# A fused Perceiver block on one core: query weights loaded first, self-attention two slots later, two products split into halves

## The reference, cut to what matters

```
x = x + cross_attention(layernorm(x), ctx)   # 16 heads, keys and values from 1601 context rows a batch
x = x + self_attention(layernorm(x))         # 8 query heads, one key and one value head of 64, causal
x = x + ffn(layernorm(x))                    # 2 shared experts, and top 2 of 8 routed ones by gates = x @ rW + rb
```

## Time and profile before

| what | before |
|---|---|
| median of 3 runs | 1284.3 us (1282.82 to 1285.09) |
| the profiled execution's own time | 1284.68 us |
| its span, first to last instruction | 1283.0 us |
| mean granted TensorE clock | 0.999 of full speed |
| PE busy | 1265.1 us, 99% of the span |
| DVE, ACT, POOL busy | 648.8, 634.0, 437.6 us |

### The profile page before, as it was taken

The page is one execution under the profiler, slowest core; times in us unless marked ns, Lnnn a source line. Parts: engine busy times, 40 slices in busy tenths (PEclk is TensorE's granted clock), DMA queues, the critical chain, the costliest instruction groups (busy, mean ns, idle before and its releaser), DMA issues.

```text
span 1283.0 us, 29915 instructions
## 1 busy us (share of the span) xinstructions
PE 1265.1 (99%) x13126; PEld 1098.9 (86%) x13126; DVE 648.8 (51%) x936; ACT 634.0 (49%) x1085; POOL 437.6 (34%) x203
## 2 busy tenths in 40 slices
PE   8999999999999999999999999999999999999998
PEld 8888888888788888788888878798989999999997
DVE  5343353443363363463453354756776555565555
ACT  3545554454545544545544536646545444554443
POOL 2345345544555545645456535200022000100000
PEclk9999999999999999999999999999999999999999
DMA  6121011012011003012003111674556499999990
GB/s 216 72 89 67 18 55 39 33 42 92 19 63 67 18 22 133 18 59 71 18 22 115 67 50 49 232 294 164 173 190 205 154 335 359 354 347 337 356 402 36
DMA packets 32775, 174.89 MB, mean 136 GB/s; under 512 B 5944, under 2 KB 8152, under 8 KB 14464
## 3 DMA queue, kind: packets, MB, share of 16 engines
q1 hardware_dynamic: 30896, 168.16, 35.6%
q0 software_dynamic: 1744, 4.76, 1.1%
HBM read 166.84 MB, written 6.06 MB: 135 GB/s over the span
## 4 chain that ended last, share of the span: by engine, by line
PE 87%; POOL 3%; DMA 3%; issue 2%; DVE 2%; ACT 2%; SPq 0%; DVEq 0%; POOLq 0%; ACTq 0%
PE bank L728 20%; PE bank L740 18%; PE bank L1079 11%; PE sc L1096 8%; PE sc L756 7%; PE sc L941 6%; PE bank L960 3%; PE bank L769 3%; PE sc L960 3%; DMA wqt<-in_aq 2%; POOL xn L587 2%; PE bank L833 1%; DMA wqt<-in_wq 1%; POOL xa L599 1%; ACT tt L1208 1%
## 5 line engine op out<-in xcount | busy, mean ns | idle before, releaser
L587 POOL TENSOR_TENSOR xn<-xn,tt 128x1024 f32<-128x1024 f32 x96 | 230.2, 2398 | 339.3 <-DVE tt L1325 338.3
L1208 ACT ACTIVATE tt<-sc 128x512 f32<-128x512 f32 (+1 forms) x208 | 107.8, 603 | 360.3 <-PE sc L756 360.2
L1423 DVE TENSOR_TENSOR wsl<-ring,wsh 128x2048 fp32r<-128x2048 f32 x72 | 166.8, 2316 | 111.6 <-ACT wsh L1163 111.1
L1312 DVE TENSOR_SCALAR kk<-bank,bkt 128x512 f32<-128x512 f32 (+2 forms) x130 | 80.8, 622 | 232.4 <-PE bank L728 232.2
L728 PE MATMUL bank<-cxh,wkh 128*128 128x512 f32 (+2 forms) x512 | 181.4, 354 | 1.5 <-DVE va L1320 1.0
L728 PE MATMUL bank<-cxl,wkh 128*128 128x512 f32 (+2 forms) x512 | 174.7, 341 | 0.0
L728 PE MATMUL bank<-cxh,wkl 128*128 128x512 f32 (+2 forms) x512 | 174.2, 340 | 0.0
L740 PE MATMUL bank<-wvh,cxh 128*128 128x512 f32 (+1 forms) x416 | 163.6, 393 | 0.0
L740 PE MATMUL bank<-wvl,cxh 128*128 128x512 f32 (+1 forms) x416 | 162.9, 391 | 0.0
L740 PE MATMUL bank<-wvh,cxl 128*128 128x512 f32 (+1 forms) x416 | 162.3, 390 | 0.0
L1163 ACT CAST wsh<-ring 128x2048 fp32r<-128x2048 f32 x72 | 137.4, 1908 | 48.2 <-PE sc L1096 20.9
(11 more groups left out here) (270 smaller groups left out, 2027.9 us busy)
## 6 DMA issues: line engine op xcount, KB each, us to landing
ring<-in_w SPq DMA_DIRECT2D x112, 1024.0 KB, 7.0
ctxt<-in_ctx SPq DMA_DIRECT2D x15, 1024.0 KB, 4.9
ctxt<-in_ctx SPq DMA_DIRECT2D x8, 642.0 KB, 3.9
ctxt<-in_ctx SPq DMA_DIRECT2D x10, 512.0 KB, 3.5
wqt<-in_wo SPq DMA_DIRECT2D x4, 1024.0 KB, 4.9
wqt<-in_aq SPq DMA_DIRECT2D x4, 1024.0 KB, 8.4
wqt<-in_ap_ SPq DMA_DIRECT2D x4, 1024.0 KB, 7.0
yrows<-K SPq DMA_DIRECT2D x1, 2048.0 KB, 9.2
```

The lines of the kernel that those rows point to most:

```text
L587: e.tensor_tensor(dacc[0:kn, y, :], dacc[0:kn, y, :], tt[0:kn, w, :], ALU.add).then_inc(s["da_pool"], 1)
L1208: e.activation(weights_view(m, kn, hb), score_read(m, kn, hb), ACT.Relu, scale=-1.0).then_inc(s["t_act"], 1)
L1423: e.tensor_tensor(wsl[m % 3][:], ring[slot(unit_split(m))][:], wsh[m % 3][:].bitcast(F32), ALU.subtract).then_inc(s["wl_dve"], 1)
```

## The change

Four edits. SP loads `in_wq` ahead of `in_wv`. `slot_of` moves every step of tiles 0 to 2 by two slots (6 becomes 8), save the gates of tile 2, which stay at slot 104. The second `halved` slot is that of step 6 instead of 5, so the split of `in_ap_` moves by three slots. The values of self-attention and the gates are made by eight products in place of four: two of 64 stationary columns each, which write PSUM partitions 0 to 63 and 64 to 127; the values are also 64 columns wide instead of 128 (the other 64 were a copy that nothing read), and so is the copy to `V2`. Both edits hold for all four tiles.

```diff
-    return next((t for t in range(3) if slot == (slot_of(t, 0) - 5, slot_of(t, 5))[what]), None)
+    return next((t for t in range(3) if slot == (slot_of(t, 0) - 5, slot_of(t, 6))[what]), None)
...
-    return 2 * PER * t + 2 * PER + 6 + (9 if d == 10 else d)
+    return 2 * PER * t + 2 * PER + 8 + (9 if d == 10 else d)
...
+            e.dma_start(wqt[:], wq).then_inc(s["wq_in"], 16)
             e.dma_start(wvt[:], wv).then_inc(s["wv_in"], 16)
-            e.dma_start(wqt[:], wq).then_inc(s["wq_in"], 16)
...
                 for c in range(4):
-                    m = e.matmul(dst[:, 0:8], xaT[:, c, :], rwt[:, c, :], start=(c == 0), stop=(c == 3))
+                    for h in range(2):
+                        r = slice(64 * h, 64 * h + 64)
+                        m = e.matmul(dst[r, 0:8], xaT[:, c, r], rwt[:, c, :], start=(c == 0), stop=(c == 3))
...
                 for c in range(4):
-                    m = e.matmul(dst[:, P:2 * P], xaT[:, c, :], avt[:, c, :], start=(c == 0), stop=(c == 3))
+                    for h in range(2):
+                        r = slice(64 * h, 64 * h + 64)
+                        m = e.matmul(dst[r, P:P + 64], xaT[:, c, r], avt[:, c, 0:64], start=(c == 0), stop=(c == 3))
...
-                e.tensor_copy(V2[:], src[:, P:2 * P]).then_inc(s["proj_read"], 1)
+                e.tensor_copy(V2[:, 0:64], src[:, P:P + 64]).then_inc(s["proj_read"], 1)
```

## The result

| what | before | after |
|---|---|---|
| median | 1283.56 us (1282.73 to 1285.09, 4 runs) | 1298.91 us (1297.9 to 1299.16, 4 runs) |
| ratio | | 1.0117 [1.0099, 1.0134] |
| span of the profiled execution | 1283.0 us | 1297.4 us |
| mean granted TensorE clock | 0.999 | 0.989 |

The account below looks back on a forecast made before the run. PE was taken as the bound, busy 1265.1 of 1283.0 us. Terms -3.5 - 2.0 + 1.4 - 3.7 + 3.2 - 2.4 = -7.0 us gave a forecast of 1277.4 us, range 1273.6 to 1282.4.

Parts of the forecast that it names:

- The step that failed: Loads of `in_ap_` and `in_wo`: claimed to have slots to spare on ACT and POOL and to cost nothing.
- (e): Rival: `context_lo` of span 0 gets behind PE at r = 10, kernel slower, some 1288 us; chance 0.05.
- The start: First loads: queries start at 15.2 instead of 16.71 us and the clock does not fall, together -3.5 us.
- the clock's 1.96 us: First sixteen query records at the start: 3.45 us at full clock instead of 5.41, a gain of 1.96 us.
- The waits of step 2, step 13 and `in_aq`: Shifted self-attention: step 2's wait gone, -2.0; step 13's grows, +1.4; `in_aq`'s gone, -3.7 us.
- The wait at `attended`: Second `attended` product waits for DVE's read of values: 1.45, 1.45 and 0.3 us, +3.2, bounds 0 and 6.0.
- The halves: Self-attention's values and gates by 64-column products side by side: 0.65 and 0.70 us, -2.4 us over four tiles.
- The gates' term: Gates made by 64-column products: 0.70 us instead of 0.95, -0.25 us a tile in four tiles.
- Rival (b): The 64-column products do not overlap: whole change -0.6 us, 1283.7 us, no change; chance 0.13.
- the dear bound: 64-column products without any overlap: 0.114 us a record, 1.8 us for values, 1.07 for gates, +3.9 us in all.
- The sum: Whole kernel: -3.5 - 2.0 + 1.4 - 3.7 + 3.2 - 2.4 = -7.0 us, forecast 1277.4 us, chance 0.52.

Follow-up runs that it names:

- e10: Changed kernel with the first split of a tile (POOL's split of wo) one slot later, residue 4 in place of 3; 1278.29 us, ratio 0.996.
- e2: Kernel before with only the output weights' split moved from r = 1 to r = 3; 1301.44 us, ratio 1.014.
- e4: Kernel before with only self-attention's values and gates made by two 64-column products side by side, with the narrower copy; 1281.38 us, ratio 0.9985.
- e5: Kernel before with only the shift by two slots, the output weights' split kept at r = 1; 1280.5 us, ratio 0.9985.
- e3: Kernel before with only the query weights loaded ahead of the value weights; 1280.94 us, ratio 0.9984.
- e6: Changed kernel with POOL's split subtraction in four instructions of 512 columns instead of one of 2048; 1290.26 us, ratio 1.0055.
- e1: Changed kernel with the output weights' split back at r = 1 instead of r = 3; 1278.11 us, ratio 0.9956.
- e12: Changed kernel with 76 idle products ahead of the value products at each of the three 4.2 us stops; 1289.35 us, ratio 1.0053.

## Why the prediction was wrong, point by point

**The step that failed** is the sentence "The loads of `in_ap_` and `in_wo` have slots to spare on ACT and POOL, and cost nothing." It is true of when the split's result is needed (`e10` delays it by another slot and loses nothing). I had looked at no more than that. I did not ask what lies on DVE beside POOL's 4.6 us, although two paragraphs on, for `attended`, I read from the earlier trace rows that an addition on POOL holds a DVE instruction until it ends. The same reading applied to the split at r = 3 gives a CAST held for some 4.4 us. This is the r = 3 of an even batch, ahead of step 0, where no step of self-attention stood between the values and the late `va`, before the change or after; `e2`, with the old places of all steps, has the same stops of 4.2 us. That is three stops, with a fallen clock behind each: by `e2`, 18 us. My description of the change names only the second number of `halved`; the first moves by two slots with `slot_of`. None of my rivals had it. My case for slower, (e), `context_lo` late at r = 10, did not happen: PE has no wait for `cxl` after.

**The start** (-3.5) went as I described in the trace after:

```profile
15.26 3.69 PE L902 MATMUL bank<-xT,wqt 128*128 128x256 f32 x16 [0.82 <-ACT xT L1133]
...
29.84 0.58 PE L740 MATMUL bank<-wvh,cxh 128*128 128x512 f32 x1
```

The first record is at 15.26 for 15.2 forecast, at full clock, and the first value product at 29.84, where it was 33.0. Alone the start measured -2.1. The term that was mis-sized is the clock's 1.96 us. I took it as sure, from one execution. The profiles of `e2`, `e4` and `e5` have the same wait, 2.3 to 2.5 us, and no fall behind it. The times of all runs say the same. Of the 19 runs of the kernel before that go with `e3`, eight lie at 1282.1 to 1282.7 and the others at 1283.6 and above; six of the ten of `e3` lie at 1280.6 to 1281.0. The lower groups are 1.5 us apart. So the 1.5 us of earlier start are there always, the 2 us only where the clock had fallen, as it had in the execution that I read.

**The waits of step 2, step 13 and `in_aq`** (-2.0, +1.4, -3.7) came as forecast: none, 2.1 in place of 0.6, none.

**The wait at `attended`** (+3.2: 1.45, 1.45, 0.3) was there with 0.9, 0.9 and none:

```profile
359.16 0.78 DVE L1464 TENSOR_TENSOR xT<-xT,bvt 128x128 f32<-128x128 f32 x1
...
363.28 0.65 PE L877 MATMUL bank<-xaT,V 64*64 64x256 f32 x4 [0.89 <-DVE va L1324]
```

POOL's hold on line 1464 is down from 1.6 to 0.5 us, by 1.1 where I had taken 0.9. The other 0.35 us I didn't trace. But a wait is not all that it costs to pull the two uses apart. From the first of them to the next group are 2.11, 2.11 and 0.94 us in `e5`, where it was 0.59 in every tile: 3.4 us more. So +3.2 was right as a price, partly by luck, since the waits are 1.8 of it. What the sum lacked is what a stop of 0.9 us can bring behind it, up to 3 us of a fallen clock.

**The halves** (-2.4, measured -1.9). The values are now 0.61 us long for 0.99, better than my 0.65. The gates take 0.64 for 0.95, but the next keys then wait for `va`:

```profile
321.68 0.69 PE L848 MATMUL bank<-avt,xaT 128*64 128x64 f32 x16
322.29 0.70 PE L756 MATMUL sc<-qc,kk 32*65 32x64 f32 x32
```

```profile
400.02 0.64 PE L812 MATMUL bank<-rwt,xaT 128*64 128x8 f32 x16
400.88 0.41 PE L728 MATMUL bank<-cxh,wkh 128*128 128x322 f32 x1 [0.22 <-DVE va L1324]
```

From the gates' start to those keys are 0.86 us, where it was 0.94. The gates' term should have been -0.1 a tile and not -0.25 in tiles 0 to 2, since DVE sets the end there. The spaces between the starts add up to -1.3 for the values and -0.5 for the gates over four tiles, which is the -1.9 measured. Sixteen records in 0.61 us are 0.038 each, so a pair of halves costs 0.076, close to line 769's 0.069. Rival (b), no overlap, is out, at 0.038 us a record for the 0.114 of the dear bound. The Trainium skill's rule that spoke for it ("TensorE: Matmul & The Clock Gate", Part 3) does not hold here: these halves load the same rows, and the measurement decides.

**The sum.** With the early split, -5.6 for -7.0 forecast, at 1278.1 for 1277.4: the rest of the sum stood, and none of its six terms had the wrong sign. What is missing fits the clock, which I counted as a sure gain at the start and left out as a possible loss at `attended`.

## What to carry to other kernels

When a number in a schedule moves, list every instruction whose place is computed from it, also those whose line the diff doesn't touch. For each long POOL instruction among them, ask what DVE does beside it, not only when its result is due. A stop of TensorE is to be priced as its length plus the clock behind it; behind stops of 4.2 and 2.9 us it fell every time that was profiled here, behind stops of 0.9 to 2.5 us in some executions and not in others, which shows as groups of times. A schedule with no stop near 1 us is worth having for its steadiness alone.

## What the runs showed of the hardware that I had not expected

- A 128x128 CAST of DVE within on-chip memory took 4.48 us beside POOL's 4.62 us subtraction, for 0.23 us alone. DVE was held until POOL's instruction ended; cut into four, it held three DVE instructions for 1.2 to 1.3 us each. A RECIPROCAL (0.94 us) and an instruction that reads PSUM (0.29 us) were not held.
- The granted clock fell at every 4.2 us stop that stayed empty (six, in the changed kernel and `e2`) and behind all three 2.9 us stops of `e6`. It fell behind a 2.2 us wait in one profile and not behind waits of 2.3 to 2.5 us in three others, and it fell behind a wait of only 0.9 us in some executions and not in others, for up to 3 us more (`e1`, `e10`, `e12` and the changed kernel against `e5`).
- 76 idle products of 128 columns in the place of each of three 4.2 us stops kept the clock up and made the kernel 9.6 us faster by the medians, 8.2 by the ratios. 7.0 us of that are the value products behind the stops.
- Two products of 64 stationary columns side by side, on all 128 rows, cost 0.076 us together (sixteen records in 0.61 us) where one of 128 columns costs 0.119.
